# MoE block kernel: two slots instead of four for one weight stream, and row statistics in pairs of token tiles

## What is computed

```
xn  = layernorm(x)                                   # x: (8, 2048, 1024) f32
v   = xn @ Wv.T + bv                                 # einsum of the softmax over m and v on the same row: rows sum to 1
att = v @ w_out.T + b_out
logits = xn @ router_w.T; top 2 of 8 experts, softmax over the two
h1  = gelu(xn @ w1[e].T + b1[e])                     # 1024 -> 4096
y_e = h1 @ w2[e].T + b2[e]                           # 4096 -> 1024
out = x + att + sum over the two chosen e of weight_e * y_e
```

## Time and profile before

| | us |
|---|---|
| runs of the kernel (slowest core) | 4110.75, 4315.02, 4233.73 (median 4233.73) |
| profiled execution, its time | 4109.1 |
| profiled execution, span of the slowest core (core 4) | 4107.1 |
| spans of the 8 cores | 4093.4 to 4107.1 |
| PE busy, share of the span | 3766.7, 92% |
| DVE / ACT / POOL busy | 355.8 / 621.7 / 667.4 |

### The profile page before, as it was taken

How to read it: one execution, slowest core, us unless ns; L and a number is a source line. 1 busy time by engine, 2 the same in 40 slices (tenths; PEclk the granted TensorE clock), 3 DMA queues, 4 the chain that set the end, 5 groups by cost and what they waited for, 6 DMA issues and landing times.

```text
span 4107.1 us, 41558 instructions; the slowest of 8 cores (4093.4 to 4107.1 us)
## 1 busy us (share of the span) xinstructions
PE 3766.7 (92%) x16857; PEld 1690.0 (41%) x17200; DVE 355.8 (9%) x626; ACT 621.7 (15%) x589; POOL 667.4 (16%) x1073
## 2 busy tenths in 40 slices
PE   3656999999999999999999999999999999999994
PEld 2222344444444444444444444444444444444442
DVE  4330110000000010100001010000000010000001
ACT  0221002030201112030202103020211202030210
POOL 1010111111111111112111111111111111111110
PEclk9787999999999999999999999999999999999997
DMA  6332445454445545455456345455554544544544
GB/s 98 69 57 39 51 71 76 72 81 66 76 71 77 75 72 75 72 77 71 75 72 147 61 72 77 70 77 70 76 75 72 76 72 76 77 71 71 77 70 107
DMA packets 255705, 307.07 MB, mean 75 GB/s; under 512 B 51687, under 2 KB 182759, under 8 KB 255520
## 3 DMA queue, kind: packets, MB, share of 16 engines
q0 software_dynamic: 248608, 279.23, 46.7%
q1 hardware_dynamic: 6912, 25.17, 1.8%
HBM read 574.89 MB, written 8.39 MB: 142 GB/s over the span
## 4 chain that ended last, share of the span: by engine, by line
PE 85%; DVE 5%; another core or an unknown queue 4%; DMA 3%; issue 2%; ACT 1%; POOL 0%; DVEq 0%; SPq 0%; ACTq 0%; POOLq 0%
PE P L381 41%; PE P L461 40%; DVE scr L475 3%; DMA wvw<-w1r 2%; PE P L411 1%; PE P L197 1%; DMA x_rot<-x 1%; ACT vg L392 1%; PE P L269 0%; POOL wvw L180 0%; DMA scr<-x 0%; DVE x_rot L505 0%; PE P L417 0%; DVEq L46 0%
## 5 line engine op out<-in xcount | busy, mean ns | idle before, releaser
L381 PE MATMUL P<-xnF,wvw 128*128 128x512 bf16 x8024 | 1798.4, 384 | 127.6 <-DMA wvw<-w1r 97.3
L461 PE MATMUL P<-wvw,vg 128*128 128x512 bf16 x8027 | 1809.7, 384 | 77.6 <-DVE scr L475 51.8
L381 PEld LDWEIGHTS P<-xnF,wvw 128*128 128x128 bf16 x8192 | 807.8, 99 | 1114.5 <-issue 176.2
L461 PEld LDWEIGHTS P<-wvw,vg 128*128 128x128 bf16 x8192 | 804.2, 99 | 1080.8 <-issue 152.7
L392 ACT ACTIVATE vg<-P,b1c_sb 128x1024 bf16<-128x1024 f32 x512 | 570.0, 1113 | 3083.7 <-PE P L381 3083.6
L438 POOL DMA_DIRECT2D wvw<-w2r x512 | 360.0, 705 | 1596.2 <-PE P L461 1521.2
L364 POOL DMA_DIRECT2D wvw<-w1r x512 | 271.7, 534 | 1409.7 <-PE P L381 1409.7
L475 DVE SCALAR_TENSOR_TENSOR scr<-P,wmap_sb,scr 128x512 f32<-128x512 f32 x256 | 192.1, 750 | 3256.1 <-PE P L461 3071.0
L180 POOL DMA_DIRECT2D wvw<-wvf x32 | 28.5, 904 | 366.7 <-PE P L285 179.4
L269 PE MATMUL P<-scr 128*128 128x128 f32 x128 | 23.8, 348 | 61.0 <-DVE scr L260 61.0
L197 PE MATMUL P<-xnF,wvw 128*128 128x512 bf16 x252 | 67.1, 414 | 11.1 <-ACT vg L392 8.7
(11 more groups left out here) (51 smaller groups left out, 141.2 us busy)
## 6 DMA issues: line engine op xcount, KB each, us to landing
wvw<-w1r POOLq DMA_DIRECT2D x512, 256.0 KB, 4.0
wvw<-w2r POOLq DMA_DIRECT2D x512, 256.0 KB, 4.1
x_rot<-x SPq DMA_DIRECT2D x28, 512.0 KB, 4.1
wvw<-wvf POOLq DMA_DIRECT2D x32, 256.0 KB, 5.0
out<-x_rot SPq DMA_DIRECT2D x16, 512.0 KB, 3.1
scr<-x SPq DMA_DIRECT2D x4, 512.0 KB, 7.3
wo_sb<-wo POOLq DMA_DIRECT2D x8, 256.0 KB, 13.9
b1c_sb<-b1c POOLq DMA_DIRECT2D x1, 128.0 KB, 14.1
```

The source lines that it names most:

```text
L381: pair=pair: t.matmul(pair[:, j * 512:(j + 1) * 512], w1sl[:, sl * 1024 + fc * 128: sl * 1024 + fc * 128 + 128], xnF[:, fc * T + half * 10 ...
L461: t.matmul(W2B[tl], vg[:, f1c * 1024 + tl * 128: f1c * 1024 + (tl + 1) * 128], w2sl[:, sl * 1024 + (f1c % 2) * 512: sl * 1024 + (f1c % 2) ...
```

## The change

`wvf_sl` shrinks from four slots to two. The load of a vp unit is emitted at the head of its own unit, not behind the matmuls of the unit four before, and waits for the unit two before. The four loads that were issued after tile 3 go. The statistics of all tiles are made in pairs of tiles ahead of their use: a pair q (tiles 2q and 2q+1) has two places in `xst` (`x_rot` is now used by the final add alone); after each odd tile the loads and the statistics of the pair q+2 are emitted, the loads waiting for the normalisation of the pair that held the place. `dcols`, `ecols`, `top2_m1` and `top2_m2` move to columns of `scr` that `xst` no longer shares. The first w2 loads of slots 0 and 1 wait for no vp unit, those of slots 2 and 3 for the last one.

The diff, cut to its core:

```diff
-    wvf_sl = wvw[:, 4096:8192]
+    wvf_sl = wvw[:, 6144:8192]
...
-    nqv = {0: 0, 1: 0, 2: 0, 3: 0}
+    nqv = {0: 0, 1: 0}
     tok_vpmm = {}
 
-    load_ord = {}
-
-    def issue_vp_load(ts, vc):
-        sl = vc % 4
-        prev = (ts, vc - 4) if vc >= 4 else (
-            (ts - 1, vc + 4) if ts >= 1 else None)
+    def emit_vp_unit(ts, vc):
+        idx = 8 * ts + vc
+        pair = SP[idx % 2]
+        sl = vc % 2
+        prev = (ts, vc - 2) if vc >= 2 else ((ts - 1, 6 + vc) if ts >= 1 else None)
         if prev is not None:
             p.wait("gpsimd", "pe", tok_vpmm[prev])
         nqv[sl] += 1
-        load_ord[(ts, vc)] = nqv[sl]
         p.do("gpsimd", lambda g, vc=vc, sl=sl: g.dma_start(
             wvf_sl[:, sl * 1024:(sl + 1) * 1024].rearrange(
                 "p (c n) -> p c n", c=NFC),
             d_wvf[vc].rearrange("c p n -> p c n")), inc=DQ[sl], inc_by=16)
-
-    def emit_vp_unit(ts, vc):
-        idx = 8 * ts + vc
-        pair = SP[idx % 2]
-        sl = vc % 4
-        if (ts, vc) not in load_ord:
-            issue_vp_load(ts, vc)
         wait_pair(idx % 2)
-        p.wait("tensor", DQ[sl], 16 * load_ord[(ts, vc)])
+        p.wait("tensor", DQ[sl], 16 * nqv[sl])
...
-        if idx + 4 < 32:
-            issue_vp_load((idx + 4) // 8, (idx + 4) % 8)
...
-    def emit_A(tt, pump, stats=None):
+    def emit_A(tt, pump, stats):
         par = tt % 2
-        if stats is None:
-            if tt >= 2:
-                p.wait("sync", "dve", tok_xnt[tt - 2])
-            nx[par] += 1
-            p.do("sync", lambda sy, tt=tt, par=par: sy.dma_start(
-                x_rot[:, par * 1024:(par + 1) * 1024],
-                d_x[tt * 128:(tt + 1) * 128, :]), inc=DX[par], inc_by=16)
-            xt = x_rot[:, par * 1024:(par + 1) * 1024]
-
-            p.wait("vector", DX[par], 16 * nx[par])
-            if tt >= 2:
-                p.wait("vector", "pe", tok_tr[tt - 2])
-            p.do("vector", lambda v, xt=xt: v.reduce_sum(st[:, 0:1], xt, axis=AX))
-            p.do("vector", lambda v: v.tensor_scalar_mul(st[:, 1:2], st[:, 0:1],
-                                                         1.0 / D))
-            p.do("vector", lambda v, xt=xt: v.scalar_tensor_tensor(
-                xsq, xt, 1.0, xt, ALU.bypass, ALU.mult, accum_out=st[:, 2:3]))
-            p.do("vector", lambda v: v.tensor_scalar_mul(st[:, 3:4], st[:, 2:3],
-                                                         1.0 / D))
-            tok_var = p.do("vector", lambda v: v.scalar_tensor_tensor(
-                st[:, 4:5], st[:, 1:2], st[:, 1:2], st[:, 3:4],
-                ALU.mult, ALU.subtract), inc="dve")
-            p.wait("scalar", "dve", tok_var)
-            p.do("scalar", lambda s: s.activation(st[:, 5:6], st[:, 4:5], AF.Ln,
-                                                  scale=-1.0, bias=eps_col))
-            tok_rstd = p.do("scalar", lambda s: s.activation(
-                st[:, 6:7], st[:, 5:6], AF.Exp, scale=-0.5), inc="act")
-            mcol, rcol = st[:, 1:2], st[:, 6:7]
-        else:
-            xt, mcol, rcol, tok_rstd = stats
-            if tt >= 2:
-                p.wait("vector", "pe", tok_tr[tt - 2])
+        xt, mcol, rcol, tok_rstd = stats
+        if tt >= 2:
+            p.wait("vector", "pe", tok_tr[tt - 2])
...
-                elif DO_B:
-                    p.wait("gpsimd", "pe", tok_vpmm[(3, 4 + sl)])
+                elif DO_B and sl >= 2:
+                    p.wait("gpsimd", "pe", tok_vpmm[(3, 7)])
...
-    p.wait("vector", "dxp", 64)
...
+    def emit_pair_prestage(q):
+        qp = q % 2
+        for t2 in range(2):
+            tt = 2 * q + t2
+            if q >= 2:
+                p.wait("sync", "dve", tok_xnt[2 * (q - 2) + t2])
+            n_dxp[qp] += 1
+            s = 2 * qp + t2
+            p.do("sync", lambda sy, tt=tt, s=s, qp=qp: sy.dma_start(
+                xst[:, s * 1024:(s + 1) * 1024],
+                d_x[tt * 128:(tt + 1) * 128, :]), inc=DXP[qp], inc_by=16)
+        dxp_need[q] = 16 * n_dxp[qp]
+
+    def emit_pair_stats(q):
+        qp = q % 2
+        p.wait("vector", DXP[qp], dxp_need[q])
+        if q >= 2:
+            p.wait("vector", "act", tok_brstd[q - 2])
+        tok = None
+        for t2 in range(2):
+            s = 2 * qp + t2
+            xt = xst[:, s * 1024:(s + 1) * 1024]
+            c = 2 * qp + t2
+            p.do("vector", lambda v, xt=xt: v.reduce_sum(st[:, 0:1], xt, axis=AX))
+            p.do("vector", lambda v, c=c: v.tensor_scalar_mul(
+                tsc[:, c:c + 1], st[:, 0:1], 1.0 / D))
+            p.do("vector", lambda v, xt=xt: v.scalar_tensor_tensor(
+                xsq, xt, 1.0, xt, ALU.bypass, ALU.mult, accum_out=st[:, 2:3]))
+            p.do("vector", lambda v: v.tensor_scalar_mul(st[:, 3:4], st[:, 2:3],
+                                                         1.0 / D))
+            tok = p.do("vector", lambda v, c=c: v.scalar_tensor_tensor(
+                tsc[:, 4 + c:5 + c], tsc[:, c:c + 1], tsc[:, c:c + 1],
+                st[:, 3:4], ALU.mult, ALU.subtract),
+                inc=(None if t2 < 1 else "dve"))
+        p.wait("scalar", "dve", tok)
+        b = 4 + 2 * qp
+        p.do("scalar", lambda s_, b=b: s_.activation(
+            tsc[:, 8 + b:10 + b], tsc[:, b:b + 2], AF.Ln,
+            scale=-1.0, bias=eps_col))
+        tok_brstd[q] = p.do("scalar", lambda s_, b=b: s_.activation(
+            tsc[:, 4 + b:6 + b], tsc[:, 8 + b:10 + b], AF.Exp,
+            scale=-0.5), inc="act")
+
+    emit_pair_prestage(0)
+    emit_pair_prestage(1)
+    emit_pair_stats(0)
+    emit_pair_stats(1)
 
     for tt in range(NTT):
-        if tt < 4:
-            emit_A(tt, pump, stats=(xst[:, tt * 1024:(tt + 1) * 1024],
-                                    tsc[:, tt:tt + 1], tsc[:, 8 + tt:9 + tt],
-                                    tok_brstd))
-        else:
-            emit_A(tt, pump)
+        q, t2 = tt // 2, tt % 2
+        qp = q % 2
+        s = 2 * qp + t2
+        emit_A(tt, pump, stats=(xst[:, s * 1024:(s + 1) * 1024],
+                                tsc[:, s:s + 1], tsc[:, 8 + s:9 + s],
+                                tok_brstd[q]))
+        if t2 == 1 and q + 2 < 8:
+            emit_pair_prestage(q + 2)
+            emit_pair_stats(q + 2)
...
-            if ts == 0:
-                for vc in range(4):
-                    issue_vp_load(0, vc)
```

More of the change, by code:

```diff
@@ L123, in build_nc @@
     p = Plan(nc)
-    p.mksem("pe", "act", "dve", "dx0", "dx1", "dq0", "dq1", "dq2", "dq3", "dw1a", "dw1b",
+    p.mksem("pe", "act", "dve", "dx0", "dx1", "dq0", "dq1", "dw1a", "dw1b",
             "dw2a", "dw2b", "dw2c", "dw2d", "dw1c", "dw1d", "dcst", "dwv",
-            "dwo", "do0", "do1", "ddbg", "dxp")
+            "dwo", "do0", "do1", "ddbg", "dxp", "dxq")
     DX = ("dx0", "dx1")
-    DQ = ("dq0", "dq1", "dq2", "dq3")
+    DQ = ("dq0", "dq1")
     DW1 = ("dw1a", "dw1b", "dw1c", "dw1d")
@@ L293, in emit_A @@
         tok_p1box[0] = emit_top2_p1(tt)
-    dcols = scr[:, 2048:2064]
-    ecols = scr[:, 2064:2080]
+    dcols = scr[:, 7296:7312]
+    ecols = scr[:, 7312:7328]
     def top2_m1(tt):
-        return scr[:, 2560 + tt * 8: 2568 + tt * 8]
+        return scr[:, 7328 + tt * 8: 7336 + tt * 8]
     def top2_m2(tt):
-        return scr[:, 2688 + tt * 8: 2696 + tt * 8]
+        return scr[:, 7456 + tt * 8: 7464 + tt * 8]
     tok_p1box = [0]
@@ L523, in pump @@
             a.pop(0)()
[L525 to L528, removed]
-    p.wait("vector", "dxp", 64)
[L530 to L547, removed]
-    for tt in range(NTT):
-        if tt < 4:
-            emit_A(tt, pump, stats=(xst[:, tt * 1024:(tt + 1) * 1024],
-                                    tsc[:, tt:tt + 1], tsc[:, 8 + tt:9 + tt],
-                                    tok_brstd))
-        else:
-            emit_A(tt, pump)
+    DXP = ("dxp", "dxq")
@@ new lines, in build_nc @@
+    n_dxp = {0: 0, 1: 0}
+    dxp_need = {}
+    tok_brstd = {}
+    def emit_pair_prestage(q):
[10 more added lines that the diff above has]
+        dxp_need[q] = 16 * n_dxp[qp]
```

## The result

| | before | after |
|---|---|---|
| profiled execution, us | 4109.1 | 4013.7 |
| its span, slowest core | 4107.1 | 4012.2 |
| all 10 runs, us | 4109.81 to 4466.12, median 4173.1 | 4011.4 to 4760.74, median 4013.55 |

The ratio of comparable runs is 0.9762 (95% interval 0.975 to 0.9774): 2.4% faster. In some executions of either kernel the cores of one die run at a lower granted clock and take some per cent longer; the comparison leaves these out, which is why the medians of all runs stand further apart than the kernels do.

A forecast was written before the change was run, and what follows sets the result against it. Ahead of the unchanged 3678.21 us, PE was taken to be held by w1 loads queued behind wvf loads. 11.6 + 48 + 63.4 - 13 = 110, less 3: span 4107.1 - 107 = 4000, plus 2.0: 4002 us, range 3972 to 4042.

The forecast's parts named there:

- the term for the clock in tiles 8, 10 and 12: 3 us taken off the gain, for matmuls that may run at 1.2 GHz behind two PE idles of about 2.5 us each.
- The mechanism: POOL's order: loads wait for units a turn back, so PE's wait for w1 (97.3 us) and the cold start go.
- Drain: h1(8) to vp23: turns without the w1 wait and cold start, 77.9 us for 141.3, a gain of 63.4.
- Tail: vp23 to vp31: two slots expose load landings of 5.0 us; 31 us for 18.0, 2 of it clock, a loss of 13.
- To h1(0): Start to first h1 group: earlier statistics, in pairs, and w1 loaded long ago; 105.0 us for 116.58, a gain of 11.6.
- Tiles 8 to 15: Stage from h1(0) to h1(8): 105.0 us for 153.0, a gain of 48, most of it from POOL's order.
- The 13.7 us from the router matmuls to a held-up vp unit: Tiles with a statistics pair in front: DVE's block, ACT's Ln and Exp, then the Gelu hold the vp unit 13.7 us.
- a sign of being wrong: Tiles 8 to 13 taking over 95 us because ACT or DVE holds them longer than 13.7 us.
- The clock rival: Remaining waits keep bringing the clock down; each of 16 groups takes 9.3 us, not 7.06: 4039 us; chance 12%.
- All behind: Everything after the tail: PE waits there for nothing the change touches, so it stays at 3678 us.

The follow-up runs named there:

- e1: The kernel before with only the new load order (two wvf slots, each load at its own unit's head), statistics as before: 4009.36 us.
- e2: The changed kernel with the old load order and its four slots put back, pair statistics kept: 4107.88 to 4115.67 us, ratio to before 1.000.
- e3: The changed kernel with four wvf slots, loads still at the head of their own unit: 3992.6 to 3994.9 us.
- e5: The changed kernel with statistics one tile at a time, four tiles ahead, Ln and Exp one tile later: 3996.0 to 3997.0 us.
- e8: The changed kernel with PE's pauses in tiles 8, 10 and 12 filled by matmuls that nobody reads: 4000.5 to 4001.9 us.
- e7: The changed kernel with four slots, single-tile statistics with late Ln and Exp, and two vp units per h1 group in the drain: 3961.7 us.
- e10: The changed kernel with the second h1 group's w1 loads held back until vp7's matmuls are done: 4011.7 to 4015.2 us.

## Why the prediction was right in its mechanism, and the step that failed

The direction, the mechanism and the drain came as forecast. The time was 4013.7 us for 4002. The step that failed is the term for the clock in tiles 8, 10 and 12: 3 us were taken off for matmuls at 1.2 GHz behind the pauses, and they cost 9.0.

- **The mechanism** (w1 loads queued behind a wvf load that waits for the newest vp unit) held. e1 and e2 show it from both sides: the order alone 4009 us, all else without it 4108 to 4116. PE waits for no w1 load ahead of an h1 group of the prologue any more.
- **Drain**: 77.9 forecast, 78.64 measured, 78.6 to 78.7 also in e1, e3, e5 and e8. The turn was built from durations of the earlier trace rows, and they came back.
- **Tail**: 31 forecast, 32.72 measured. The landing was 4.8 us (5.0 taken). The clock's part was set too low: 2 us for 1.2 GHz matmuls, 3.8 measured (units of 2.35, 3.57 and 3.57 us for 1.89), while on the slowest cores of the kernels with the same tail it took 36.4 (e8), 38.3 (e5) and 38.9 us (e1), with a clock of 0.73 to 0.84. That core 1 took 32.72, of 30.7 to 37.1 on the eight cores, made this term look better than it was. Two slots make this stretch longer and less steady than I had it.
- **To h1(0)**: 105.0 forecast, 107.46 measured on the slowest core; the wait ahead of vp7 was 5.26 us and not 0.9. I gave the load 5 us; it took 9.7 on this core and 4.4 on core 0. w1 was not loaded long before, as I wrote: it was issued at 94.84, behind vp7's load, but in time. And the gain was put down to the wrong cause. I added it up from earlier statistics, and the first transposes did come 6 us sooner (23.62 for 29.62). But the kernel before had PE free for h1(0) at 107.1 us, so 9.5 of the 11.6 us forecast are its wait for w1, and e1 has them with the old statistics. That the number came out near was partly luck. A slip besides: with the 7.0 us for each tile that the text gives, tiles 0 to 3 and the statistics between them come to 57.25 us, not 57.6.
- **Tiles 8 to 15**, the largest miss, 112.05 for 105.0 and 3. This is the step that failed, the term for the clock. I allowed 3 us for cold matmuls behind the pauses. Three vp units at 3.57 for 1.89 and two groups at 9.29 and 8.85 for 7.07 make 5.0 + 4.0 = 9.0. The arithmetic of waits was right, and 2 us too dear: e8, where the clock stays up, took 103.0 us for the 105.0 that the waits alone gave. The 13.7 us from the router matmuls to a held-up vp unit were 14.2 in tile 10 (137.9 to 152.09). Tiles 8 to 13 took 90.9 us, 82.9 forecast, and so stayed under the 95 that I had named as a sign of being wrong.
- **The clock rival** (each of 16 groups cold, 4039) was the wrong form of it. In the drain, with waits of 0.98 and 1.52 us by turns, the clock stays at 1.00; in tiles 8 and 10, where a pause of 2.75 to 3.55 us and another of 1.34 to 2.63 lie close together, the unit and the group behind them are slow. The rule in the Trainium skill, page "TensorE: Matmul & The Clock Gate", section "A second HAM failure mode: psum-queue depth-cycling", that frequent short idles between matmul groups which cycle through PSUM make the clock go up and down, isn't borne out by the drain of this kernel: waits of 0.98 and 1.52 us by turns, 78.64 us long, and a granted clock of 1.00.
- **All behind**: taken as unchanged, 3 us more. The same code took 3674.6 to 3681.3 us in the profiled executions of e1, e3, e7, e8 and the changed kernel, so differences of this size can't be put down to the change.
- **Against which time**: the forecast, 4002 us, was made against 4109.1 and is a change of 2.6%; measured are 2.4%. Beside the median of the first three runs (4233.73) the same forecast reads as 5.5%, more than twice what was measured, and no part of the sum supports that.

## What to carry to other kernels

On a queue that runs strictly in order, a prefetch that waits for the newest consumer blocks every load behind it, however early these could have gone: issue it where what it waits for is already past, and buffers may then be fewer, not more. Count a pause of the tensor engine twice, once for itself and once for the matmuls behind it that run at half the clock; here the second part was forecast at 3 us and took 9, beside about 13 for the pauses themselves. Work that needs small loads should lie between work that needs none of them: taking two vp units for each group did as much here as doubling the slots. And compare a core with the same core of the other execution: the slowest was core 1 in the changed kernel and core 3 in e10, and from one to the other a wait seemed to shrink that hadn't on either.

## What the runs showed of the hardware

- A pause of PE of 3.55 us, eight transposes and another of 2.63 us took the granted clock from 1.00 to 0.51 in tile 10, and it cost 1.7 us in the unit and 1.8 in the group behind it. In tile 12 the same pair slowed only the unit (3.57 us; the group took 7.07). Waits of 0.98 and 1.52 us by turns, through 78.64 us, left the clock at 1.00.
- Matmuls whose result nobody reads, put in PE's pauses, kept the clock at 1.00 and made tiles 8 to 15 9 us faster (103.0 for 112.05).
- A 256 KB load issued first in a burst of six landed after 4.4 to 4.7 us on cores 0, 2, 4 and 6 and after 7.6 to 9.7 on cores 1, 3, 5 and 7 of the same execution, for a median of 4.8 in the tail. In e10, with four loads in the burst, it was 4.5 to 4.6 on cores 1, 2, 4 and 6 and 7.2 to 8.7 on cores 0, 3, 5 and 7. In five profiled executions one core of each pair of neighbours was late, never both and never none.
